# One-hot chunks of a product-key decoder layer in pairs, scores in one piece, and a quarter of the gates moved from GpSimd to VectorE

## The reference

```python
xn = (x - mean) * rsqrt(var + EPS) * bn_gamma + bn_beta          # batch statistics over all tokens
q = (xn @ w_q.T).reshape(b, s, 2, NH, KD)                        # NH = 8 heads, KD = 128
sim = einsum('pbnhd,hkpd->pbnhk', q, keys_p)                     # two sets of NK = 64 keys
scores, idx = top_k(sim, K)                                      # K = 8 in each set
all_scores = scores[0][..., :, None] + scores[1][..., None, :]   # 64 sums, indices idx0 * 64 + idx1
sc, pk = top_k(all_scores, K)                                    # the 8 best experts of a head
hmid = sigmoid(sc) * gelu(einsum('bnd,bnhkd->bnhk', inputs, down[indices]))
out = einsum('bnhk,bnhkd->bnd', hmid, up[indices])
x = layernorm(x + out)
```

## Time and profile before

| | before |
|---|---|
| median of 3 runs | 2992.36 us (2992.18 to 2992.92) |
| profiled execution | 2992.0 us |
| its span | 2990.3 us |
| mean granted TensorE clock | 0.949 |
| TensorE matmul busy | 2686.5 us (90%) |
| TensorE weight load busy | 2289.4 us (77%) |
| VectorE busy | 2228.6 us (75%) |
| GpSimd busy | 796.4 us (27%) |
| ScalarE busy | 741.4 us (25%) |

### The profile page before, as it was taken

One profiled execution on the slowest core, in us unless ns is written; L12 is line 12 of the kernel. 1 busy time (PEld: TensorE's weight loads), 2 busy tenths in 40 slices (PEclk: granted clock), 3 DMA queues, 4 the chain that ended last, 5 costly groups with the idle time before them and its releaser, 6 DMA issues.

```text
span 2990.3 us, 104463 instructions
## 1 busy us (share of the span) xinstructions
PE 2686.5 (90%) x43108; PEld 2289.4 (77%) x43108; DVE 2228.6 (75%) x7540; ACT 741.4 (25%) x1302; POOL 796.4 (27%) x604
## 2 busy tenths in 40 slices
PE   7961066689999999999999999999999999999996
PEld 5841054578888888888888888888888888888895
DVE  5668976577777777777777777777777777777754
ACT  4730044222222222222222222222222222222210
POOL 1330000033333333333333333333333333333332
PEclk9985588899999999999999999999999999999997
DMA  5560047500000000000000000000000000000000
GB/s 174 174 175 0 0 123 178 104 2 13 13 13 13 13 13 13 13 13 13 13 13 13 13 13 13 13 13 13 13 13 13 13 13 13 13 13 13 9 10 12
DMA packets 84639, 99.52 MB, mean 33 GB/s; under 512 B 6189, under 2 KB 74702, under 8 KB 84046
## 3 DMA queue, kind: packets, MB, share of 16 engines
q1 hardware_dynamic: 84190, 92.94, 10.9%
HBM read 65.13 MB, written 27.79 MB: 31 GB/s over the span
## 4 chain that ended last, share of the span: by engine, by line
PE 80%; issue 1%; DVE 1%; DMA 0%; SPq 0%; ACT 0%; POOL 0%; DVEq 0%; ACTq 0%; POOLq 0%
PE bank L1001 31%; PE bank L1030 30%; PE bank L1016 9%; PE bank L977 8%; DVE hot L1207 1%; PE bank L966 1%; PE bank L989 1%; DMA gelh<-in_table 0%; SPq L926 0%; DVE gelh L1219 0%; POOL hot L948 0%; DVE top_i L1163 0%; PE bank L1044 0%; DVE top L1159 0%; DVE yo L1226 0%
## 5 line engine op out<-in xcount | busy, mean ns | idle before, releaser
L948 POOL TENSOR_TENSOR hot<-hot,valsT 128x512 f32<-128x512 f32 x512 | 732.8, 1450 | 2011.3 <-DVE hot L1207 2011.3
L1001 PE MATMUL bank<-x2T,dnT 128*64 128x128 f32 x16384 | 952.0, 274 | 2.5 <-issue 2.1
L1030 PE MATMUL bank<-up,gelh 64*128 64x256 f32 x8192 | 911.9, 379 | 1.5 <-DVE gelh L1219 1.5
L1001 PEld LDWEIGHTS bank<-x2T,dnT 128*64 128x64 f32 x16384 | 891.3, 137 | 26.8 <-issue 14.0
L1030 PEld LDWEIGHTS bank<-up,gelh 64*128 64x128 f32 x8192 | 787.0, 187 | 140.5 <-issue 50.8
L1207 DVE TENSOR_TENSOR hot<-iota,valsT 128x1024 f32<-128x1024 f32 x512 | 647.9, 1306 | 28.2 <-ACT valsT L1106 28.2
L1219 DVE TENSOR_TENSOR gelh<-bank,gelh 128x512 f32<-128x512 f32 x512 | 329.8, 686 | 239.5 <-PE bank L1016 234.1
L1111 ACT ACTIVATE gelh<-bank 128x512 f32<-128x512 f32 x512 | 299.1, 597 | 682.9 <-PE bank L1001 682.2
L1016 PE MATMUL bank<-hot 64*64 64x64 f32 x16384 | 307.2, 224 | 40.0 <-issue 23.6
L1016 PEld LDWEIGHTS bank<-hot 64*64 64x64 f32 x16384 | 270.2, 137 | 91.1 <-issue 91.1
L1159 DVE MAX8 top<-bank 128x8 f32<-128x64 f32 x1024 | 140.9, 220 | 265.2 <-PE bank L977 256.9
(11 more groups left out here) (143 smaller groups left out, 1873.5 us busy)
## 6 DMA issues: line engine op xcount, KB each, us to landing
x_scratch<-x_sb SPq DMA_DIRECT2D x64, 256.0 KB, 2.2
xT_sb<-in_xT SPq DMA_DIRECT2D x32, 256.0 KB, 2.9
x_sb<-in_x SPq DMA_DIRECT2D x32, 256.0 KB, 2.9
x_again<-x_scratch SPq DMA_DIRECT2D x32, 256.0 KB, 2.8
x_tile<-x_scratch SPq DMA_DIRECT2D x32, 256.0 KB, 3.7
up<-in_table SPq DMA_DIRECT2D x2, 4096.0 KB, 40.4
yo<-x_scratch SPq DMA_DIRECT2D x32, 256.0 KB, 2.8
out_y<-yo SPq DMA_DIRECT2D x32, 256.0 KB, 2.0
```

What stands on the lines that cost most here:

```text
L948: pool.tensor_tensor(lo, lo, valsT[:, par, 2, TQ * q:TQ * (q + 1), None].to_broadcast([P, TQ, NK]), ALU.mult).then_inc(gated_ready, 1)
L1001: mm = pe.matmul(ps_h[q % 2][half(c), i, :], dnT[:, k, lo // 2, half(lo % 2)], x2T[:, k, c, :], start=(k == 0), stop=(k == CC - 1))
L1030: mm = pe.matmul(ps_out[c], gelh[half(c), par, lo, :], up[half(c), lo, :], start=(lo == 0), stop=(lo == NK - 1))
```

## The change

TensorE does two coefs in a run and then four hidden; an even coefs writes to banks 5 and 6, an odd one to banks 0 and 1. Both turns stand behind coefs 5, the turn of tokens goes to bank 7, and x2T has two buffers. Both scores of a group stand between the last hidden and the output, which is in one piece; the first half's scores go to banks 0 and 1, the second half's to banks 3 and 4. VectorE makes four slots in a run, then the products of two coefs. Of each four slots GpSimd gates three and VectorE gates the fourth, behind a drain. In the opening score(0, 1) stands ahead of the transposes of the table (which use two banks), the scores of group 1 stand ahead of hidden(0) in banks of their own, turn_vals(0) comes in the middle of hidden(0), and route(1, 0) ahead of the first slots. The constants iota8 and the first 64 columns of iota become one tile, places.

```diff
             x2T = se("x2T", [P, 2, CC, 2, P])
+            ps_score = (bank[0], bank[1]), (bank[3], bank[4])
+            ps_score1 = (bank[5], bank[6]), (bank[2], bank[7])
+            ps_xT = bank[7][:, :].rearrange("p (k n) -> p k n", k=CC)
+            ps_vals0 = bank[5][:, 0:3 * P].rearrange("p (v t) -> p v t", v=3)
-            ps_a = [bank[5 + i] for i in range(2)]
+            ps_a = [(bank[5], bank[6]), (bank[0], bank[1])]
+            ps_dn = [bank[5 + i][:, :].rearrange("p (k c e) -> p k c e", k=CC, c=2) for i in range(2)]
...
# GpSimd
-                    pool.wait_ge(hot_ready, g * NQ + (q + 1))
+                    pool.wait_ge(hot_ready, g * 12 + (3 * (q // 4) + q % 4 + 1))
...
                     for q in range(NQ):
-                        gated(g, par, q)
+                        if q % 4 < 3:
+                            gated(g, par, q)
...
# TensorE: score, hidden, coefs, output
+                    if later(g, 2):
+                        pe.wait_ge(scores_read, 2 * g)
+                        if a:
+                            pe.wait_ge(gel_ready, g * NQ)
+                        else:
+                            pe.wait_ge(coef_ready, NA * (g - 1))
...
+                    if q < 2:
+                        pe.wait_ge(scores_read, 2 * g + 2)
...
-                    pe.wait_ge(gated_ready, g * NQ + 2 * (n + 1))
-                    if later(g, 1) or n:
-                        pe.wait_ge(coef_ready, g * NA + n)
+                    pe.wait_ge(gated_ready, g * 12 + 3 * (n // 2) + 2 + n % 2)
+                    if n % 2:
+                        pe.wait_ge(gated_last, g * 4 + (n // 2 + 1))
+                    if n >= 2:
+                        pe.wait_ge(coef_ready, g * NA + (n - 1))
+                    elif later(g, 1):
+                        pe.wait_ge(coef_ready, g * NA + (n - 1))
+                        pe.wait_ge(scores_read, 2 * g + (3 if within(g, 1) else 2))
...
+                    if within(g, 2):
+                        pe.wait_ge(x2T_ready, g + 3)
+                        pe.wait_ge(xn_ready, g + 3)
...
# TensorE: opening
                 turn(0, 0)
                 score(0, 0)
+                score(0, 1)
                 for q in range(NQ):
...
+                turn(1, 1)
                 pe.wait_ge(dnT_ready, NQ)
-                score(0, 1)
+                score(1, 0)
+                score(1, 1)
                 for q in range(NQ):
-                    hidden(0, q)
-                turn(1, 1)
-                score(1, 0)
-                turn_vals(0)
-                score(1, 1)
+                    hidden(0, 0, q)
+                    if q == 7:
+                        turn_vals(0)
...
# TensorE: step
-                    for n in range(NA):
-                        coefs(g, n)
-                        if n == 5 and within(g, 1):
+                    for m in range(NA // 2):
+                        coefs(g, 2 * m)
+                        coefs(g, 2 * m + 1)
+                        if m == 2 and within(g, 1):
                             turn_vals(g + 1)
-                        if n == NA - 1 and within(g, 2):
-                            turn(g + 2, par)
+                            if within(g, 2):
+                                turn(g + 2, par)
                         if within(g, 1):
-                            hidden(g + 1, 2 * n)
-                            hidden(g + 1, 2 * n + 1)
-                    output(g, par, range(0, 8))
+                            for q in range(4 * m, 4 * m + 4):
+                                hidden(g + 1, 1 - par, q)
                     if within(g, 2):
                         score(g + 2, 0)
-                    output(g, par, range(8, 24))
-                    if within(g, 2):
                         score(g + 2, 1)
-                    output(g, par, range(24, NK))
+                    output(g, par)
...
# ScalarE: step
-                        if q == 11 and within(g, 1):
-                            vals_cols(g + 1, 1 - par)
-                        if q == NQ - 1 and within(g, 2):
-                            norm_in(g + 2)
+                        if q == 8:
+                            if within(g, 1):
+                                vals_cols(g + 1, 1 - par)
+                            if within(g, 2):
+                                norm_in(g + 2)
+                                raw_in(g + 2, par)
...
# VectorE: hots
+                    both = dve.tensor_tensor(hot[:, q % SLOTS], places[:, None, None, :].to_broadcast([P, 2, TQ, NK]),
                                       valsT[:, par, 0:2, TQ * q:TQ * (q + 1), None].to_broadcast([P, 2, TQ, NK]),
-                                      ALU.is_equal).then_inc(hot_ready, 1)
+                                      ALU.is_equal)
+                    if q % 4 < 3:
+                        both.then_inc(hot_ready, 1)
+                    else:
+                        dve.drain()
+                        lo = hot[:, q % SLOTS, 1]
+                        dve.tensor_tensor(lo, lo, valsT[:, par, 2, TQ * q:TQ * (q + 1), None].to_broadcast([P, TQ, NK]),
+                                          ALU.mult).then_inc(gated_last, 1)
...
# VectorE: opening and step
                 route(0, 0)
                 route(0, 1)
+                route(1, 0)
                 for q in range(SLOTS):
                     hots(0, 0, q)
-                route(1, 0)
                 route(1, 1)
...
-                    for n in range(NA):
-                        coefs(g, par, n)
-                        if n == 0 and later(g, 1):
-                            norm(g - 1)
-                        if n == 3 and later(g, 1):
-                            scale(g - 1)
-                        for q in (2 * n + SLOTS, 2 * n + SLOTS + 1):
+                    for m in range(NA // 2):
+                        for q in range(4 * m + SLOTS, 4 * m + SLOTS + 4):
                             if q < NQ:
                                 hots(g, par, q)
                             elif within(g, 1):
                                 hots(g + 1, 1 - par, q - NQ)
+                        coefs(g, par, 2 * m)
+                        coefs(g, par, 2 * m + 1)
+                        if m == 0 and later(g, 1):
+                            norm(g - 1)
+                        if m == 1 and later(g, 1):
+                            scale(g - 1)
```

More of the change, by code:

```diff
@@ L897, in half, with scores_of, vals_of @@
                 return slice(H2 * i, H2 * (i + 1))
+            def scores_of(g, a):
+                return ps_score1[a] if isinstance(g, int) and g == 1 else ps_score[a]
+            def vals_of(g):
+                return ps_vals0 if isinstance(g, int) and g == 0 else ps_vals
             def within(g, n):
@@ L960, in turn @@
                     if later(g, 1):
-                        pe.wait_ge(scores_read, 2 * g)
                         pe.wait_ge(x2T_ready, g)
                         pe.wait_ge(xn_ready, g)
+                    if isinstance(g, int) and g == 2:
+                        pe.wait_ge(scores_read, 4)
+                    if later(g, 3):
+                        pe.wait_ge(sum3_done, g - 2)
                     for k in range(CC):
@@ L983, in turn_vals @@
                     pe.wait_ge(gate_ready, 2 * (g + 1))
+                    if isinstance(g, int) and g < 2:
+                        pe.wait_ge(scores_read, 3 + g)
                     if later(g, 1):
@@ L1000, in hidden @@
                             for c in range(2):
-                                mm = pe.matmul(ps_h[q % 2][half(c), i, :], dnT[:, k, lo // 2, half(lo % 2)], x2T[:, k, c, :],
+                                mm = pe.matmul(ps_h[q % 2][half(c), i, :], dnT[:, k, lo // 2, half(lo % 2)], x2T[:, par, k, c, :],
                                                start=(k == 0), stop=(k == CC - 1))
@@ L1015, in coefs @@
                                 q = 2 * n + at // TQ
-                                mm = pe.matmul(ps_a[a][half(c), t * NK:(t + 1) * NK],
+                                mm = pe.matmul(ps_a[n % 2][a][half(c), t * NK:(t + 1) * NK],
                                                hot[half(a), q % SLOTS, 0, at % TQ, :], hot[half(a), q % SLOTS, 1, at % TQ, :],
@@ L1019, in coefs, with output @@
                     mm.then_inc(a_mm, 1)
[L1021 to L1028, removed]
+                def output(g, par):
+                    pe.wait_ge(coef_ready, NA * (g + 1))
+                    if within(g, 1):
+                        pe.wait_ge(valsT_ready, g + 2)
+                    if within(g, 2):
+                        pe.wait_ge(x2T_ready, g + 3)
+                        pe.wait_ge(xn_ready, g + 3)
+                    if later(g, 1):
+                        pe.wait_ge(sum3_done, g)
+                    for lo in range(NK):
                         for c in range(2):
@@ L1158, in route @@
                         for h in range(NH):
[L1159 removed]
```

(3 more changed lines are left out.)

68 lines of the change are left out of this document (34 added, 34 removed).

## The result

The changed kernel takes 3133.32 us (median of 4 runs, 3128.53 to 3136.63) against 2992.27 for the kernel before on the same chip (4 runs): ratio 1.0472, 95% interval 1.0454 to 1.049, slower by 141 us. The forecast was 3134. The profiled execution has a span of 3134.8 against 2990.3.

A forecast was written before the change was run, and what follows sets the result against it. VectorE's chain was to bound each group ahead of the scores, TensorE the scores and output. Opening -24, groups 29*5.33, last two groups +6.0 and +4.4 give +141 on 2992.4: 3134 us, range 3085 to 3190.

The forecast's parts named there:

- The deciding step, VectorE's block: Four slots in turns with GpSimd, then VectorE's gate, before the products: 7.70 us, or 7.1 without the shared-read exclusion.
- The chain of a group: First coefs to next group: TensorE waits for VectorE's products at C2, C4, C6 and scores; 79.77 us against 74.44.
- the same instructions in the same order stand in every block: VectorE's runs of four slots: each takes 6.32 us like the one traced in the opening, not 4.6.
- The loop's 0.47: Groups 1 to 29: the loop's back edge and a few slips add 0.47 us to an undisturbed group.
- TensorE's part: Coefs, hidden, scores and output: two coefs and four hidden take 9.21 us, not 9.47; own work falls about 1.7 a group.
- rival 1: GpSimd finds gaps without holding up VectorE; TensorE bounds the group at 73.9 us, total 2952, faster; chance 0.11.
- ScalarE's part: Runs of four hidden leave gelu's table loads uncovered: 0.58 us twice a group, 1.16 in all.
- The ends: Opening gains 24 us (bounds 10 to 32); group 30 loses 6.0 and group 31 loses 4.4.
- 2: Rival: TensorE's clock falls behind its waits, each group's output starting at half clock; +88 us, 3222; chance 0.07.
- 3: Rival: VectorE's gate slips in ahead of GpSimd's third; block 7.1 us, 2.4 less a group, 3062; chance 0.05.

The follow-up runs named there:

- experiment 2: Changed kernel with GpSimd writing ones over a slot's second matrix instead of gating it, so it reads no SBUF tile: 2985.26 us, ratio 0.9982.
- experiment 1: Changed kernel with the fourth gate of each block given back to GpSimd, so all gates are on GpSimd: 2989.35 us, ratio 0.9993.
- 3: Changed kernel with VectorE's earlier order (products of one coefs, two slots, products of the next, two slots), gates as changed: 3003.84 us, ratio 1.0042.
- 6: Kernel before the change, with only every fourth gate moved to VectorE behind a drain: 2998.75 us, ratio 1.002.
- kernel 8: Changed kernel with VectorE's earlier order, all gates on GpSimd and gelu's table loaded early: 2970.93 us, ratio 0.9922.
- experiments 1 to 4: Four runs on the changed kernel; the fourth has VectorE's earlier order and all gates on GpSimd: 2981.37 us, ratio 0.9972.
- experiment 7: Changed kernel with gelu's table loaded early, by a one-column gelu behind the square root and behind the sigmoids: 3137.99 us, ratio 1.0483.
- experiment 9: As kernel 8, but TensorE's coefs and hidden in the earlier order, one coefs and two hidden eight times: 2939.48 us, ratio 0.9822.
- experiment 5: Changed kernel with one small tensor_scalar on VectorE ahead of each run of four slots: 3079.59 us, ratio 1.029.

## Why the prediction was right, point by point

- **The deciding step, VectorE's block.** Right, and shown: 7.70 forecast and measured; taking turns (experiment 2) and the gate that stands ahead of the products (1 and 3) are each needed for the loss. The price isn't in the gate itself: it costs nothing in the old order (6).
- **The chain of a group.** Right to 0.5: C2 10.47 (forecast 10.37), C4 22.47 (22.32), C6 32.80 (33.31), S 44.46 (44.88), S S O 34.9 (34.89). The step that failed is "the same instructions in the same order stand in every block": the block behind the scale takes 6.00. By the working that would bring C6 to 31.6, but TensorE then comes last (no wait stands at 1650.89), so an undisturbed group takes 79.32, and only 0.45 of the 1.70 was saved.
- **The loop's 0.47.** The mean of 80.25 lies 0.93 above the undisturbed 79.32. Of that 0.60 is the loop's (the first group of a round takes 80.57 on average), so this term was a little small. The other 0.33, 9.5 us in all, are the six groups with a spell of half clock, which the working put at nothing. These errors cancel the 0.45 saved; the 80.25 against a forecast of 80.24 is partly luck.
- **TensorE's part.** The pitch of C C H H H H holds (C2 comes 9.18 behind C0 in the second groups of kernel 8, 9.21 forecast). The group does so only by luck: rival 1's 73.9 has 1.16 of gelu in it, and kernel 8 takes 74.00 without gelu's waits, because its second pair of coefs waits 0.82 for GpSimd's gates, a wait that the working put at nothing. And C C H H H H brings gaps that the working didn't have. In the changed kernel VectorE's chain covers most of them. In rival 1's world they don't hide: its 2952 would have been 2985 (experiment 2), and experiments 1 to 4 came out 9 to 37 us above what was expected; the longer first groups of a round are a good part of it.
- **ScalarE's part.** TensorE's waits for gelu were there (23.9 us over the span, mostly 0.3 to 0.5 each), and covered, as the chain said: experiment 7 takes part of them away and gains nothing. The price where nothing covers them was too high: 1.16 a group in the working, 0.45 by experiment 8.
- **The ends.** Opening -24.8 (forecast -24). Group 30 +8.0 (forecast +6.0) and group 31 +6.5 (forecast +4.4): together 4 short. Group 30 stands just behind the loop, and C2 comes 11.85 behind C0 there for a gap of 1.14 in its first coefs that nothing seen explains; a spell of half clock brings C6 to 35.35, 2.0 later than forecast, and that is group 30's part. In the last group TensorE is at half clock (a run of 128 at 3.69), which the forecast had allowed for; new is that VectorE stands idle for 1.06 amid its first products, again with nothing seen to wait for, and C2 comes 11.58 behind C0.
- **The rivals.** 1: slots take turns, out. 2: the mean clock of the groups stays near 1.00, so it is out at its price of 88 us, but not in kind: behind waits of up to 2.24 us the clock does fall in 6 of groups 1 to 29, at 1.5 to 1.7 us each. 3: VectorE's gate is 1.37 in the mean, not 0.69, out. In the block behind the scale the slots are free and GpSimd is held up, yet VectorE's gate takes 1.38 there too (at 1647.10).

Where the 141 went, then: 7 us a group of VectorE's chain ahead of the scores, less 1.7 of TensorE's saving. The same edits without the run of four, without VectorE's gate and without paired coefs, and with gelu's table loaded early (experiment 9), are 53 us faster than before.

## What to carry to other kernels

Before moving work onto an engine with slack, write out the chain from one release to the next: slack over a group (here 5 us) says nothing if the moved work stands between a wait and what that wait feeds. Put the products that another engine waits for ahead of the refill of the buffers, not behind it. And when TensorE's order is rebuilt for a count of saved changeovers, look in the trace for "issue" gaps behind the loop's back edge before believing the count.

## What the runs showed of the hardware

- **A run of slots keeps its free pace behind a tensor_scalar.** Four slots took 4.62 and not 6.33 in the 30 blocks that followed the scale without idle time, in 20 of experiment 1, and in 61 of 63 in experiment 5 that so followed the small tensor_scalar; then GpSimd's first gate waits instead (three gates last 6.58 and not 5.82 in the rows above). Behind any idle time (0.03 is the shortest in experiment 1, 0.02 in experiment 5) the effect is gone. The Trainium skill (SBUF — State Buffer, Who interferes with whom) has the exclusion, which the turns agree with, but by it alone this block would be like the others. Why VectorE keeps the reads is open.
- **TensorE has gaps without a cause in the trace behind a loop's back edge, and more of them when short matmuls stand close.** With C H H there is one gap a round, which makes its first group 0.9 to 1.1 longer; with C C H H H H there are three to five, about 2 us a round. In the loop's first round, which no jump back leads to, the gaps at records 30 and 155 are missing. That short matmuls in a row (64 records in 1.16 us, twice as many with C C) are taken faster than instructions arrive behind the jump fits this, but it was only argued: no run changed the supply alone.
